# First attention of a two-layer transformer: order of the score and weighting steps on TensorE, and the normalisation on VectorE

## The chip, the cores and the metric

The kernel runs on one core of one Trainium2 chip. The metric is the device time of one execution in microseconds (us).

## The reference, cut to what matters

The whole program is two layers, each an attention and a feed-forward part. The change touches the first attention alone: 16 heads of width 16, two batches of 2048 tokens, causal.

```python
q, k, v = heads(x @ Wq.T), heads(x @ Wk.T), heads(x @ Wv.T)
scores = jnp.einsum('bhqd,bhkd->bhqk', q, k) / sqrt(d_k) + mask
attn = jax.nn.softmax(scores, axis=-1)
out = jnp.einsum('bhqk,bhkd->bhqd', attn, v)
```

## The kernel before, in words

`phase_attention` works through eight units. A unit is four heads of one batch. Inside a unit the 2048 queries are four slices of 512 (q = 0 to 3), and the keys are tiles of 128 (t). By causality slice q needs key tiles 0 to 4q+3, so a unit has 4+8+12+16 = 40 steps (q, t), numbered g = 0 to 39. The last four steps of a slice lie on the diagonal. There the first `off` = 0, 128, 256, 384 columns are masked in full and are left out, so these four steps are 512, 384, 256 and 128 queries wide. All other steps are 512 wide. A slice edge is therefore a passage from the narrowest step to a full one: g3 to g4, g11 to g12, g23 to g24, and g39 to g0 of the next unit.

Each step does this:

- TensorE computes scores in two pairs of heads (p = 0, 1), two matmuls a pair, into one of three `ps_s` buffers (L758). Pair s = 2*step+p may start once the exponential of pair s-3 has released its buffer.
- ScalarE takes the exponential of a pair, 128 x up to 1024 elements, from PSUM into one of four `probs` buffers (L710). A step's first exponential waits for the weighting of the step four back.
- On diagonal steps GpSimd zeroes the triangle of the 128 x 128 block in all four heads (L698).
- TensorE "weighs": it multiplies probs by V with a column of ones, four heads side by side, and accumulates in `ps_o[:, q % 2]` (L775). Row 16 of each head's 32 rows is the sum of the exponentials.

At the end of a slice VectorE copies `ps_o` to `weighted` (L723), splits it into a high and a low part (L725, L727). TensorE spreads the sums over the rows of their head by two matmuls into the same `ps_o` buffer (L788, L789). VectorE takes the reciprocal (L730), multiplies (L732) and splits the result (L736, L738). SyncE writes it out. The first weighting of slice n waits for VectorE's reading of the spread totals of slice n-2, which held the same `ps_o` buffer.

Nothing schedules this: each engine's order is written out in Python. On TensorE the order is set by `LAG = 2`: scores of step `at`, weighting of step `at - 2`, and the spread of a slice that ended at step `at - 4`.

```python
for at in range(len(STEPS) + LAG + 2):
    if at < len(STEPS):
        scores(at)
    if 0 <= at - LAG < len(STEPS):
        weigh(at - LAG)
    if at - LAG - 2 >= 0:
        u, g = STEPS[at - LAG - 2]
        if g in LAST:
            spread_denominators(u, LAST.index(g))
```

Of the kernel before, what the change touches and what calls it, by code (L numbers as in the profile page):

```python
# [15 lines left out]
P = 128  # L16
# [5 lines left out]
BT = TB * P  # L22
# [9 lines left out]
HALF = 64  # L32
STACK_ROWS = 3 * DH
SHIFT_PARTS = 2
USED_ROWS = STACK_ROWS + SHIFT_PARTS
# [25 lines left out]
def sems(k, stem, names):  # L61
    return [sem(k, f"{stem}_{n}") for n in names.split()]
# [547 lines left out]
def phase_attention(k):  # L610
# [6 lines left out]
    TILE_LIST = [(q, t, max(0, (t - TB * q) * P)) for q in range(SLICES) for t in range(TB * (q + 1))]  # L617
    NT = len(TILE_LIST)
    LAST = [max(g for g, (q, _, _) in enumerate(TILE_LIST) if q == s) for s in range(SLICES)]
    DIAG = [g for g, (q, t, _) in enumerate(TILE_LIST) if t >= TB * q]  # L620
    STEPS = [(u, g) for u in range(UNITS) for g in range(NT)]
    SCORE_BUFS, PROB_BUFS = 3, 4
    LAG = 2
    LOADS = STACK_LOADS + 2
    ROWS_OUT = 2 * HG

    with ExitStack() as mem:
        def sb(name, shape, dt):
            return mem.enter_context(nc.sbuf_tensor(name, shape, dt))

        Q, K = ((k["first_stacks"][n], sb(name, [P, 2, SEQ], F32R)) for n, name in enumerate(("Q_odd", "K_odd")))
# [3 lines left out]
        inv = sb("inv_denominator", [P, BT], F32)  # L635
# [4 lines left out]
        ps_s = mem.enter_context(nc.psum_tensor("ps_s", [P, SCORE_BUFS, 2, BT], F32))  # L640
        ps_o = mem.enter_context(nc.psum_tensor("ps_o", [P, 2, BT], F32))
# [3 lines left out]
        ones_in, pick_ok, zero_ok, scores_ok, exp_ok, mask_ok, pv_ok, sums_ok, picked_ok, norm_ok, result_ok = sems(  # L645
            k, "attention", "ones_in pick_ok zero_ok scores_ok exp_ok mask_ok pv_ok sums_ok picked_ok norm_ok result_ok")

        def group_and_batch(u):
            return u % GROUPS, u // GROUPS

        with nc.Block() as block:
# [14 lines left out]
            @block.sync  # L666
            def _(sp):
                load_shifts(sp, 0, 0)
                load_ones(sp, io, K[1], ones_in)
                load(sp, 1, 1)  # L670
                for u in range(UNITS):
                    g, b = group_and_batch(u)
                    for q in range(SLICES):
                        sp.wait_ge(result_ok, SLICES * u + q + 1)
                        for n, out in enumerate((out_hi, out_lo)):
                            for h in range(HG):
                                row = HG * DH * g + DH * h
                                sp.dma_start(io["attended"][n, b, row:row + DH, q * BT:(q + 1) * BT],
                                             out[32 * h:32 * h + DH, q % 2].bitcast(F32)).then_inc(stored[q % 2], 16)
                    if u + 2 < UNITS:  # L680
                        sp.wait_ge(scores_ok, 2 * NT * (u + 1))
                        load(sp, u + 2, u % 2)
                for j in range(2):
                    sp.wait_ge(stored[j], 16 * ROWS_OUT * (SLICES // 2 * UNITS))
# [28 lines left out]
            @block.vector  # L713
            def _(dve):
                dve.memset(ps_o[:, :, :], 0.0).then_inc(zero_ok, 1)
                dve.sem_inc(loaded[0], 16 * STACK_LOADS)
                dve.wait_ge(pick_ok, 2)
                dve.tensor_copy(pick[:, :, :], pick_f32[:, :, :]).then_inc(pick_ok, 1)
                for u in range(UNITS):
                    for q in range(SLICES):  # L720
                        n = SLICES * u + q
                        dve.wait_ge(pv_ok, NT * u + LAST[q] + 1)
                        dve.tensor_copy(sums[:, q % 2], ps_o[:, q % 2]).then_inc(sums_ok, 1)  # L723
                        dve.wait_ge(sums_ok, 3 * n + 1)
                        dve.tensor_copy(sums_hi[:, :], sums[:, q % 2]).then_inc(sums_ok, 1)  # L725
                        dve.wait_ge(sums_ok, 3 * n + 2)
                        dve.tensor_tensor(sums_lo[:, :], sums[:, q % 2], sums_hi[:, :].bitcast(F32), ALU.subtract  # L727
                                          ).then_inc(sums_ok, 1)
                        dve.wait_ge(picked_ok, n + 1)
                        dve.reciprocal(inv[:, :], ps_o[:, q % 2]).then_inc(norm_ok, 1)  # L730
                        dve.wait_ge(norm_ok, 3 * n + 1)
                        dve.tensor_tensor(result[:, :], sums[:, q % 2], inv[:, :], ALU.mult).then_inc(norm_ok, 1)  # L732
                        dve.wait_ge(norm_ok, 3 * n + 2)
                        if n >= 2:
                            dve.wait_ge(stored[q % 2], 16 * ROWS_OUT * (n // 2))
                        dve.tensor_copy(out_hi[:, q % 2], result[:, :]).then_inc(norm_ok, 1)  # L736
                        dve.wait_ge(norm_ok, 3 * n + 3)
                        dve.tensor_tensor(out_lo[:, q % 2], result[:, :], out_hi[:, q % 2].bitcast(F32), ALU.subtract  # L738
                                          ).then_inc(result_ok, 1)

            @block.tensor
            def _(pe):
                pe.wait_ge(zero_ok, 1)

                def scores(at):
                    u, g = STEPS[at]
                    j = u % 2
                    q, t, off = TILE_LIST[g]
                    if g == 0:
                        pe.wait_ge(loaded[j], 16 * LOADS * (u // 2 + 1))  # L750
                        if u == 1:
                            pe.wait_ge(ones_in, 32)
                    for p in range(2):
                        s = 2 * at + p
                        if s >= SCORE_BUFS:
                            pe.wait_ge(exp_ok, s - SCORE_BUFS + 1)
                        for h in range(2):
                            last = pe.matmul(ps_s[:, s % SCORE_BUFS, h, off:BT],  # L758
                                             K[j][HALF * h:HALF * h + USED_ROWS, p, t * P:(t + 1) * P],
                                             Q[j][HALF * h:HALF * h + USED_ROWS, p, q * BT + off:(q + 1) * BT],  # L760
                                             start=True, stop=True)
                        last.then_inc(scores_ok, 1)

                def weigh(at):
                    u, g = STEPS[at]
                    q, t, off = TILE_LIST[g]
                    group, b = group_and_batch(u)
                    n = SLICES * u + q
                    if t == 0 and n >= 2:
                        pe.wait_ge(norm_ok, 3 * (n - 2) + 1)  # L770
                    pe.wait_ge(exp_ok, 2 * at + 2)
                    if g in DIAG:
                        pe.wait_ge(mask_ok, len(DIAG) * u + DIAG.index(g) + 1)
                    for h in range(HG):
                        last = pe.matmul(ps_o[32 * h:32 * h + DH + 1, q % 2, off:BT],  # L775
                                         k["V"][:, group, SEQ_TILES * b + t, h, :],
                                         probs[:, at % PROB_BUFS, h, off:BT],
                                         start=(t == 0), stop=(g == LAST[q]))
                    last.then_inc(pv_ok, 1)

                def spread_denominators(u, q):

                    n = SLICES * u + q
                    if n == 0:
                        pe.wait_ge(pick_ok, 3)
                    pe.wait_ge(sums_ok, 3 * n + 3)
                    rows = pick[:, :, :].rearrange("p h r -> p (h r)")
                    pe.matmul(ps_o[:, q % 2], rows, sums_hi[:, :], start=True, stop=False)  # L788
                    pe.matmul(ps_o[:, q % 2], rows, sums_lo[:, :], start=False, stop=True).then_inc(picked_ok, 1)  # L789

                for at in range(len(STEPS) + LAG + 2):
                    if at < len(STEPS):
                        scores(at)
                    if 0 <= at - LAG < len(STEPS):
                        weigh(at - LAG)
                    if at - LAG - 2 >= 0:
                        u, g = STEPS[at - LAG - 2]
                        if g in LAST:
                            spread_denominators(u, LAST.index(g))

# [1333 lines left out]
```

## Time and profile before

| quantity | value |
|---|---|
| median of 3 runs | 1855.95 us (1855.9 to 1857.81) |
| the profiled execution | 1856.14 us |
| its span, first to last instruction | 1854.3 us |
| mean granted TensorE clock, of full speed | 0.943 |
| first attention: first and last exponential | 124.3 us and 672.3 us of the span |
| busy in the whole span: TensorE, ScalarE, VectorE, GpSimd | 88%, 52%, 50%, 25% |

The span is read from the first to the last instruction; the profiled execution took 1.8 us more. The first attention is 548 us of it. Times in the rows further down count from the start of the span.

### The profile page before, as it was taken

What the parts mean: (1) busy time and instruction counts of PE and PEld (TensorE: products, weight loads), DVE (VectorE), ACT (ScalarE), POOL (GpSimd) and SP (SyncE); (2) the same over time, 40 slices, a digit from 0 to 9 for tenths busy, and PEclk for the clock granted to TensorE, in tenths of its full rate; (3) what the DMA queues carried; (4) which work ended last, traced back from release to release, by engine and by line L of the source; (5) the groups of instructions that cost most, each with busy time, mean ns of one, the idle gap of its engine ahead of it and who ended that gap; (6) DMA issues with size and microseconds to landing.
All of it is one profiled execution on the core that took longest, in us unless ns stands there. A gap on an engine that the chain in (4) does not pass through costs nothing. (4 is left out here: it accounts for less than half of the span.)

```text
span 1854.3 us, 30959 instructions
## 1 busy us (share of the span) xinstructions
PE 1626.1 (88%) x10275; PEld 1110.3 (60%) x10276; DVE 922.7 (50%) x1795; ACT 962.0 (52%) x1531; POOL 457.7 (25%) x500
## 2 busy tenths in 40 slices
PE   7769999999999957999559999999668987997998
PEld 5632322322322316888548888888567976896887
DVE  6524433443443436777553333333375554755785
ACT  5459999999999944443332222222133334333332
POOL 0001111210210201555542222222153003001674
PEclk9979999999999987999879999999878997998999
DMA  8991405514514029221231111111212010000001
GB/s 274 268 254 28 86 14 88 87 24 77 87 30 70 18 62 308 79 80 46 76 107 50 50 50 51 51 51 51 88 46 91 1 57 1 1 1 4 24 23 46
DMA packets 79647, 134.44 MB, mean 73 GB/s; under 512 B 11632, under 2 KB 46064, under 8 KB 76400
## 3 DMA queue, kind: packets, MB, share of 16 engines
q1 hardware_dynamic: 72504, 112.00, 23.4%
q0 software_dynamic: 7040, 21.08, 3.6%
q8 instruction: 64, 1.05, 0.2%
q14 instruction: 39, 0.32, 0.1%
HBM read 74.76 MB, written 58.27 MB: 72 GB/s over the span
## 5 line engine op out<-in xcount | busy, mean ns | idle before, releaser
L710 ACT ACTIVATE probs<-ps_s 128x1024 f32<-128x1024 f32 (+3 forms) x640 | 513.8, 954 | 37.2 <-PE ps_s L758 34.2
L775 PE MATMUL ps_o<-probs,V 128*17 128x512 f32 (+3 forms) x2560 | 297.4, 536 | 0.3
L698 POOL TENSOR_SCALAR_AFFINE_SELECT probs<-probs 128x512 f32<-128x512 f32 x128 | 86.8, 680 | 465.5 <-ACT probs L710 461.9
L723 DVE COPY weighted<-ps_o 128x512 f32<-128x512 f32 x32 | 22.1, 690 | 254.7 <-PE ps_o L775 254.7
L1389 DVE COPY slot_hT<-ps_hT 128x512 f32<-128x512 f32 x72 | 49.8, 691 | 196.7 <-PE ps_hT L1432 196.7
L758 PEld LDWEIGHTS ps_s<-Q_even,K_even 50*128 50x128 f32 x640 | 56.1, 186 | 152.1 <-ACT probs L710 130.0
L730 DVE RECIPROCAL inv_denominator<-ps_o 128x512 f32<-128x512 f32 x32 | 107.4, 3358 | 73.8 <-PE ps_o L789 73.8
L758 PE MATMUL ps_s<-Q_even,K_even 50*128 50x512 f32 (+3 forms) x640 | 127.6, 446 | 18.8 <-DMA Q_even<-shift_parts 10.5
L758 PEld LDWEIGHTS ps_s<-Q_odd,K_odd 50*128 50x128 f32 x640 | 55.2, 183 | 140.0 <-ACT probs L710 125.8
L1442 PE MATMUL ps_slot_y<-we_out,slot_hT 128*128 x576 | 136.5, 380 | 1.4 <-DVE slot_hT L1389 0.9
L1922 POOL TENSOR_TENSOR h_lo<-h,h_hi 128x512 fp32r<-128x512 f32 x64 | 89.4, 1413 | 183.8 <-DVE h L1968 183.8
L758 PE MATMUL ps_s<-Q_odd,K_odd 50*128 50x512 f32 (+3 forms) x640 | 126.6, 442 | 7.8 <-ACT probs L710 6.3
L1347 POOL DMA_INDIRECT routed_rows<-slot_y,home_row x72 | 70.3, 977 | 181.5 <-ACT slot_y L1366 176.9
L1808 ACT ACTIVATE probs<-ps_s,neg_row_max 128x512 f32<-128x512 f32 (+2 forms) x80 | 49.3, 623 | 121.2 <-DVE neg_row_max L1770 121.2
L1442 PEld LDWEIGHTS ps_slot_y<-we_out,slot_hT 128*128 128x128 f32 x576 | 103.9, 190 | 13.3 <-issue 2.0
L117 PE MATMUL ps_slot_mid<-we_in_hi,slot_xT_hi 128*128 x144 | 69.6, 483 | 22.8 <-DVE slot_xT_lo L1393 22.8
L775 PEld LDWEIGHTS ps_o<-probs,V 128*17 128x17 f32 x2560 | 42.7, 95 | 77.0 <-issue 63.5
L1371 ACT ACTIVATE slot_silu<-ps_slot_mid 128x512 f32<-128x512 f32 x72 | 43.1, 598 | 80.0 <-PE ps_slot_mid L119 80.0
L1366 ACT ACTIVATE slot_y<-ps_slot_y 128x256 f32<-128x256 f32 x72 | 27.6, 384 | 106.6 <-PE ps_slot_y L1442 106.6
L117 PE MATMUL ps_o<-v_hi,pT_hi 128*128 128x256 f32 x272 | 80.9, 297 | 2.2 <-DVE pT_lo L1775 2.0
L1361 ACT ACTIVATE slot_xT_hi<-ps_xT 128x256 fp32r<-128x256 f32 x72 | 27.6, 384 | 105.1 <-PE ps_xT L1419 105.1
L974 POOL DMA_INDIRECT slots_in<-scaled_rows,slot x64 | 66.3, 1036 | 57.4 <-DVE scaled_rows L1105 42.3
(279 smaller groups left out, 3950.2 us busy)
## 6 DMA issues: line engine op xcount, KB each, us to landing
qk_stacks<-qk_hi SPq DMA_DIRECT2D x64, 256.0 KB, 3.9
slot_rows<-slots_in SPq DMA_DIRECT2D x72, 128.5 KB
qk_stacks<-qk_lo SPq DMA_DIRECT2D x32, 256.0 KB, 3.9
Q_odd<-qk_stacks SPq DMA_DIRECT2D x8, 768.0 KB
K_odd<-qk_stacks SPq DMA_DIRECT2D x8, 768.0 KB
Q_even<-qk_stacks SPq DMA_DIRECT2D x6, 768.0 KB
K_even<-qk_stacks SPq DMA_DIRECT2D x6, 768.0 KB
X<-x SPq DMA_DIRECT2D x8, 512.0 KB, 4.4
```

The source lines that it names most:

```text
L117: pe.matmul(out, lh, rh, start=start, stop=False)
L698: pool.affine_select(out=block_of, in_=block_of, compare_op=ALU.is_ge, fill=0.0, base=0, pattern=[[0, HG], [1, P]], channel_multiplier=-1) ...
L710: act.activation(probs[:, at % PROB_BUFS, 2 * p:2 * p + 2, off:BT], ps_s[:, s % SCORE_BUFS, :, off:BT], ACT.Exp).then_inc(exp_ok, 1)
L730: dve.reciprocal(inv[:, :], ps_o[:, q % 2]).then_inc(norm_ok, 1)
L758: last = pe.matmul(ps_s[:, s % SCORE_BUFS, h, off:BT], K[j][HALF * h:HALF * h + USED_ROWS, p, t * P:(t + 1) * P], Q[j][HALF * h:HALF * h + ...
L775: last = pe.matmul(ps_o[32 * h:32 * h + DH + 1, q % 2, off:BT], k["V"][:, group, SEQ_TILES * b + t, h, :], probs[:, at % PROB_BUFS, h, off ...
L974: pool.indirect_dma_start(out=io["slots_in"], out_offset=bass.IndirectOffsetOnAxis(ap=k["slot"][:, r, TB * b + t:TB * b + t + 1], axis=0), ...
L1347: pool.indirect_dma_start(out=io["routed"], out_offset=bass.IndirectOffsetOnAxis(ap=home[:, j], axis=0), in_=y[:, j, :], in_offset=None).t ...
L1389: dve.tensor_copy(hT[:, :, :], ps_h[:, :, :]).then_inc(hT_ok, 1)
L1442: last = pe.matmul(ps_y[:, :], hT[:, f], wo[:, bass.ds(e, 1), f, :], start=(f == 0), stop=(f == FC - 1))
L1808: act.activation(probs[:, q % 2, g * P:(g + m) * P], ps_s[:, g * P:(g + m) * P], ACT.Exp, bias=neg_top[:, q:q + 1], accum_out=chunk_total[ ...
L1922: pool.tensor_tensor(h_lo[:, j, f], h[:, f % 2], h_hi[:, j, f].bitcast(F32), ALU.subtract).then_inc(lo_ok, 1)
```

## The change

It does two things. On TensorE, `LAG` is replaced by a table: before the weighting of step `at`, scores are issued up to pair 2*at+1 plus 4 where the step is 512 or 128 wide, and plus 6 where it is 384 or 256 wide. The spread of a slice stays two weightings behind its last one. On VectorE, the spread totals are first copied from PSUM to SBUF (`inv_denominator`), and the reciprocal is taken in place from the copy; the semaphore that releases the `ps_o` buffer is raised by the copy.

```diff
-    LAG = 2
+    LEAD = {0: 4, P: 6, 2 * P: 6, 3 * P: 4}
+    SPREAD_AFTER = 2
...
-                        dve.reciprocal(inv[:, :], ps_o[:, q % 2]).then_inc(norm_ok, 1)
-                        dve.wait_ge(norm_ok, 3 * n + 1)
+                        dve.tensor_copy(inv[:, :], ps_o[:, q % 2]).then_inc(norm_ok, 1)
+                        dve.wait_ge(norm_ok, 4 * n + 1)
+                        dve.reciprocal(inv[:, :], inv[:, :]).then_inc(norm_ok, 1)
+                        dve.wait_ge(norm_ok, 4 * n + 2)
...
-                        pe.wait_ge(norm_ok, 3 * (n - 2) + 1)
+                        pe.wait_ge(norm_ok, 4 * (n - 2) + 1)
...
-                for at in range(len(STEPS) + LAG + 2):
+                scored = 0
+                for at in range(len(STEPS) + SPREAD_AFTER):
                     if at < len(STEPS):
-                        scores(at)
-                    if 0 <= at - LAG < len(STEPS):
-                        weigh(at - LAG)
-                    if at - LAG - 2 >= 0:
-                        u, g = STEPS[at - LAG - 2]
+                        for s in range(scored, min(2 * at + 2 + LEAD[TILE_LIST[STEPS[at][1]][2]], 2 * len(STEPS))):
+                            scores(s)
+                            scored = s + 1
+                        weigh(at)
+                    if at >= SPREAD_AFTER:
+                        u, g = STEPS[at - SPREAD_AFTER]
```

TensorE's order before, at the start of a unit, from the scores of g2 (256 wide) to those of g6. `ps_s` rows are scores, `ps_o` rows with `probs` are weightings, L788 and L789 the spread of the last slice of the unit before.

```order
L758 MATMUL ps_s<-Q_odd,K_odd 128x256 x4
L775 MATMUL ps_o<-probs,V 17x512 x4
L758 MATMUL ps_s<-Q_odd,K_odd 128x128 x4
L775 MATMUL ps_o<-probs,V 17x384 x4
L788 MATMUL ps_o<-weighted_hi,denominator_pick 128x512
L789 MATMUL ps_o<-weighted_lo,denominator_pick 128x512
L758 MATMUL ps_s<-Q_odd,K_odd 128x512 x4
L775 MATMUL ps_o<-probs,V 17x256 x4
L758 MATMUL ps_s<-Q_odd,K_odd 128x512 x4
L775 MATMUL ps_o<-probs,V 17x128 x4
L758 MATMUL ps_s<-Q_odd,K_odd 128x512 x4
```

The same place in the changed kernel, where the same lines are L760, L777, L790 and L791:

```order
L760 MATMUL ps_s<-Q_odd,K_odd 128x256 x4
L777 MATMUL ps_o<-probs,V 17x512 x4
L760 MATMUL ps_s<-Q_odd,K_odd 128x128 x4
L760 MATMUL ps_s<-Q_odd,K_odd 128x512 x4
L777 MATMUL ps_o<-probs,V 17x384 x4
L790 MATMUL ps_o<-weighted_hi,denominator_pick 128x512
L791 MATMUL ps_o<-weighted_lo,denominator_pick 128x512
L760 MATMUL ps_s<-Q_odd,K_odd 128x512 x4
L777 MATMUL ps_o<-probs,V 17x256 x4
L777 MATMUL ps_o<-probs,V 17x128 x4
L760 MATMUL ps_s<-Q_odd,K_odd 128x512 x4
```

The scores of g4, the first full step of the next slice, have moved ahead of the weighting of g1 and of the spread; those of g5 ahead of the weighting of g2; and the weightings of g2 and g3 now follow each other. The same happens at the other three slice edges, where no spread stands in between. Away from the edges the order is the old one.

VectorE's order for one slice, in the changed kernel:

```order
L724 COPY weighted<-ps_o 128x512 [waits attention_pv_ok]
L726 CAST weighted_hi<-weighted 128x512 [waits attention_sums_ok]
L728 TENSOR_TENSOR weighted_lo<-weighted,weighted_hi 128x512 [waits attention_sums_ok]
L731 COPY inv_denominator<-ps_o 128x512 [waits attention_picked_ok]
L733 RECIPROCAL inv_denominator<-inv_denominator 128x512 [waits attention_norm_ok]
L735 TENSOR_TENSOR attention_result<-weighted,inv_denominator 128x512 [waits attention_norm_ok]
L739 CAST attention_hi<-attention_result 128x512 [waits attention_norm_ok]
```

Before, one RECIPROCAL from `ps_o` (L730) stood where the COPY and the RECIPROCAL now are; the rest is as it was.

## Rows read from the trace of the kernel before

**Rows 1.** Busy time by stretch: window, PE, PEld, DVE, ACT, POOL, clock, DMA share, GB/s.
```profile
124.30:193.50 69.20, 67.01 (x472) 20.22 (x470) 21.25 (x21) 64.22 (x81) 10.64 (x16) 0.95 0.31 53
330.60:399.00 68.40, 66.04 (x490) 20.30 (x488) 28.14 (x28) 64.22 (x80) 10.93 (x17) 1.00 0.38 63
```
**Rows 2.** The page's groups: line, operation, count | busy, mean ns | idle before, releaser.
```profile
L710 ACT ACTIVATE probs<-ps_s 128x1024 f32<-128x1024 f32 (+3 forms) x640 | 513.8, 954 | 37.2 <-PE ps_s L758 34.2
...
L723 DVE COPY weighted<-ps_o 128x512 f32<-128x512 f32 x32 | 22.1, 690 | 254.7 <-PE ps_o L775 254.7
...
L730 DVE RECIPROCAL inv_denominator<-ps_o 128x512 f32<-128x512 f32 x32 | 107.4, 3358 | 73.8 <-PE ps_o L789 73.8
```
**Rows 3.** ScalarE's waits, 330.6 to 399: total us, times, longest.
```profile
ACT probs L710 <- PE ps_s L758: 3.8, 5, 1.4
```
**Rows 4.** Timeline of ScalarE around 349 us: start us, us, line, operation, count, idle before.
```profile
347.48 1.81 ACT L710 ACTIVATE probs<-ps_s 128x768 f32<-128x768 f32 x3
349.39 0.66 ACT L710 ACTIVATE probs<-ps_s 128x256 f32<-128x256 f32 x2
350.70 1.02 ACT L710 ACTIVATE probs<-ps_s 128x1024 f32<-128x1024 f32 x1 [0.65 <-PE ps_s L758]
```
**Rows 5.** Timeline of TensorE around 349 us.
```profile
349.33 0.84 PE L775 MATMUL ps_o<-probs,V 128*17 128x384 f32 x8
```
**Rows 6.** Timeline of TensorE in the unit's first 14 us.
```profile
334.58 0.44 PE L758 MATMUL ps_s<-Q_odd,K_odd 50*128 50x128 f32 x4
335.04 0.84 PE L775 MATMUL ps_o<-probs,V 128*17 128x384 f32 x8
335.81 0.50 PE L788 MATMUL ps_o<-weighted_hi,denominator_pick 128*128 128x512 f32 x1
336.47 0.73 PE L758 MATMUL ps_s<-Q_odd,K_odd 50*128 50x512 f32 x4
...
343.69 0.50 PE L788 MATMUL ps_o<-weighted_hi,denominator_pick 128*128 128x512 f32 x1 [0.40 <-DVE weighted_lo L727]
```
**Rows 7.** Timeline of ScalarE around 335 us.
```profile
333.80 1.12 ACT L710 ACTIVATE probs<-ps_s 128x512 f32<-128x512 f32 x2
335.01 0.38 ACT L710 ACTIVATE probs<-ps_s 128x256 f32<-128x256 f32 x1
337.07 1.02 ACT L710 ACTIVATE probs<-ps_s 128x1024 f32<-128x1024 f32 x1 [1.41 <-PE ps_s L758]
```
**Rows 8.** Timeline of VectorE from the reciprocal of the unit before.
```profile
336.58 3.36 DVE L730 RECIPROCAL inv_denominator<-ps_o 128x512 f32<-128x512 f32 x1 [2.18 <-PE ps_o L789]
...
341.77 0.68 DVE L723 COPY weighted<-ps_o 128x512 f32<-128x512 f32 x1
```
**Rows 9.** Single lines of VectorE: duration ns min/median/max, first and last start.
```profile
L1793 DVE RECIPROCAL inv_row_sum<-row_sum x32: 163/164/166, 1395.9 to 1695.3; 128x1 f32<-128x1 f32 x32
...
L215 DVE RECIPROCAL ln_rstd<-ln_std x32: 166/170/180, 9.9 to 1815.6; 128x4 f32<-128x4 f32 x32
...
L725 DVE CAST weighted_hi<-weighted x32: 426/426/428, 134.7 to 674.3; 128x512 fp32r<-128x512 f32 x32
...
L736 DVE CAST attention_hi<-attention_result x32: 426/428/740, 143.1 to 680.4; 128x512 fp32r<-128x512 f32 x32
```
**Rows 10.** Timeline of TensorE in unit 0.
```profile
129.38 0.69 PE L758 MATMUL ps_s<-Q_even,K_even 50*128 50x128 f32 x4
130.00 1.48 PE L775 MATMUL ps_o<-probs,V 128*17 128x384 f32 x8
```
**Rows 11.** Timeline of ScalarE in unit 0, after the same scores.
```profile
132.03 3.77 ACT L710 ACTIVATE probs<-ps_s 128x1024 f32<-128x1024 f32 x4 [1.47 <-PE ps_s L758]
```
**Rows 12.** Timeline of VectorE at the end of the attention.
```profile
676.29 3.36 DVE L730 RECIPROCAL inv_denominator<-ps_o 128x512 f32<-128x512 f32 x1 [0.82 <-PE ps_o L789]
...
693.52 0.43 DVE L152 CAST wo_hi<-silu 128x512 fp32r<-128x512 f32 x1 [11.96 <-DMA router_raw<-router]
```
**Rows 13.** Timeline of GpSimd at the next diagonal.
```profile
346.97 0.63 POOL L698 TENSOR_SCALAR_AFFINE_SELECT probs<-probs 128x512 f32<-128x512 f32 x1 [10.60 <-ACT probs L710]
```

More of the change, by code:

```diff
@@ L729, in _ @@
                         dve.wait_ge(picked_ok, n + 1)
-                        dve.reciprocal(inv[:, :], ps_o[:, q % 2]).then_inc(norm_ok, 1)
-                        dve.wait_ge(norm_ok, 3 * n + 1)
+                        dve.tensor_copy(inv[:, :], ps_o[:, q % 2]).then_inc(norm_ok, 1)
+                        dve.wait_ge(norm_ok, 4 * n + 1)
+                        dve.reciprocal(inv[:, :], inv[:, :]).then_inc(norm_ok, 1)
+                        dve.wait_ge(norm_ok, 4 * n + 2)
                         dve.tensor_tensor(result[:, :], sums[:, q % 2], inv[:, :], ALU.mult).then_inc(norm_ok, 1)
-                        dve.wait_ge(norm_ok, 3 * n + 2)
+                        dve.wait_ge(norm_ok, 4 * n + 3)
                         if n >= 2:
@@ L736, in _ @@
                         dve.tensor_copy(out_hi[:, q % 2], result[:, :]).then_inc(norm_ok, 1)
-                        dve.wait_ge(norm_ok, 3 * n + 3)
+                        dve.wait_ge(norm_ok, 4 * n + 4)
                         dve.tensor_tensor(out_lo[:, q % 2], result[:, :], out_hi[:, q % 2].bitcast(F32), ALU.subtract
@@ L743, in _, with scores @@
                 pe.wait_ge(zero_ok, 1)
-                def scores(at):
+                def scores(s):
+                    at, p = s // 2, s % 2
                     u, g = STEPS[at]
@@ L748, in scores @@
                     q, t, off = TILE_LIST[g]
-                    if g == 0:
+                    if g == 0 and p == 0:
                         pe.wait_ge(loaded[j], 16 * LOADS * (u // 2 + 1))
@@ L752, in scores @@
                             pe.wait_ge(ones_in, 32)
[L753 to L762, printed above, removed]
+                    if s >= SCORE_BUFS:
+                        pe.wait_ge(exp_ok, s - SCORE_BUFS + 1)
+                    for h in range(2):
+                        last = pe.matmul(ps_s[:, s % SCORE_BUFS, h, off:BT],
+                                         K[j][HALF * h:HALF * h + USED_ROWS, p, t * P:(t + 1) * P],
+                                         Q[j][HALF * h:HALF * h + USED_ROWS, p, q * BT + off:(q + 1) * BT],
+                                         start=True, stop=True)
+                    last.then_inc(scores_ok, 1)
                 def weigh(at):
```

## The prediction

> **What bounds the kernel now.** The change touches one stage, so I first read the busy times by stretch [rows 1]. The second row is one unit of the first attention: in 68.40 us ScalarE is busy 64.22 and TensorE 66.04. TensorE's figure overstates it, because overlapping matmuls are counted from start to modelled end. Its clock is at 1.00, the 2.4 GHz level, in that unit and at 0.95 in unit 0. Next the page's groups [rows 2]: the exponentials at L710 stand for 513.8 us, and ScalarE idles 37.2 us before them, nearly all for scores at L758. That makes ScalarE the bound, with its stalls as the prize. ScalarE's waits show how few they are: 5 in one unit, 3.8 us together, the longest 1.4 [rows 3]. Four stand where a slice's narrow steps end, and the fifth at the second slice's last full step. All work between them runs at ScalarE's own pace, and the change does not alter it.
>
> **Part 1, scores earlier at a slice edge.** I take the edge from g11 to g12. The last narrow exponential starts at 349.39+0.66-0.38 = 349.67, with 0.38 for one of them [rows 7]; the two start 0.66-0.38 = 0.28 apart. The next, g12's first, starts only at 350.70 [rows 4]. Its own buffer had been released when g10's second exponential ended, at 347.48+1.81 = 349.29. Between the two stands the weighting of g9, which TensorE started at 349.33 for 0.84 us [rows 5]. Now the scores go first. One pair takes 0.50, as a spread matmul of the same 512 columns does, and ScalarE follows 0.10 later: g4's scores start at 336.47, and 336.47+0.50 = 336.97 stands against its exponential at 337.07 [rows 6, 7]. From a release to the start of what waits for it I allow 0.05 (my estimate; VectorE's reciprocal follows the spread by 0.04). So 349.29+0.65 = 349.94. ScalarE itself could start 0.28 after 349.67, at 349.95. So g12 starts at 349.95 instead of 350.70, which is 0.75 us less. The edges into g24 and into g0 of the next unit show the same wait of 0.65. Over 8 units that is 8 + 8 + 7 = 23 edges: 23 x 0.75 = **-17.3 us**.
>
> Does the wait come back one step later? g13's first exponential needs a free `probs` buffer, that is the weighting of g9, which now stands behind g12's scores. It ended at 350.17 [rows 5], and even 1 us later it ends before 351.8, when g13's exponential is due (349.95 + 2 x 0.92; four full ones take 3.77 with 1.02 for one, so they follow each other every 0.92 [rows 4, 11]). I count nothing for it.
>
> **Part 2, the edge from g3 to g4.** Here the spread of the unit before stands in the queue too, and ScalarE waits longest, 1.41 us [rows 7]. Now g4's scores need only the release by g2's second exponential at 333.80+1.12 = 334.92, so its first exponential starts at about 335.57 instead of 337.07. This gain does not last: g8, the last full step of this slice, is held from the other side. Its scores stand behind the spread of slice 0, and that spread waits 0.40 us for VectorE [rows 6]. VectorE is late because it still works on the slice before: the reciprocal starts at 336.58, and only when three more operations are done does it copy slice 0, at 341.77 [rows 8]. What decides g8 is thus how VectorE's chain moves, by two terms.
>
> First, the chain starts later. The spread moves behind g4's scores. These end at about 335.95 (the release by g3's first exponential at 335.01+0.38, plus 0.05, plus 0.50). The weighting of g1 then takes 0.84 and the spread 0.73, with each start 0.07 ahead of the end before it, as 335.81 is of 335.04+0.84 = 335.88; so the spread ended at 336.47+0.07 = 336.54, 0.73 after its start [rows 6]. Now: 335.95-0.07+0.84-0.07+0.73 = 337.38, against 336.54. That is +0.84 us.
>
> Second, the chain changes length. A copy from PSUM costs 0.69 [rows 2] and the wait between the two some 0.035 (an estimate, after the 0.04 from 336.54 to the reciprocal's start at 336.58 [rows 8]). The reciprocal from PSUM took 3.36. **The price of a reciprocal from SBUF at this width is not in the trace**, and it decides the case. The upper end is that it costs the same, 3.36. The lower end comes from the small ones: 164 ns for one element, 170 for four [rows 9], so 2 ns for each further element where the PSUM form needs (3358-164)/511 = 6.25; 164+511 x 2 = 1.19 us. At 6.25 ns per element the four-element form would take 183 ns, and none of its 32 runs took over 180. A middle value comes from copies: from PSUM 690 ns [rows 2], as a cast between SBUF tensors 426 [rows 9], so about half per element once a fixed part of some 160 is taken off. Half of the reciprocal's element time gives 164+3194/2 = 1761 ns. I take 1.76: it lies nearer to the small rows than the upper end does. The Trainium skill agrees with the halving: "VectorE: DVE Perf Modes", section "Why PSUM operands drop a tier", says that the doubled two-port mode needs both SBUF read ports and PSUM has one. It names no reciprocal, so it does not settle whether this operation has such a mode; if none, the sum is that of the second rival.
>
> With 1.76 the chain is 0.69+0.035+1.76-3.36 = -0.87, and -0.87+0.84 = -0.03: g8 starts where it did. In units 1 to 7: 7 x -0.03 = **-0.2 us**.
>
> **Unit 0** has no chain before it and a low clock at its start. The scores of g3 end at 130.07, and those of g4 stand behind a weighting of 1.48 [rows 10]; g4's exponential starts at 132.03 [rows 11]. Without that weighting in front, its scores take some 0.7 from 130.0: 130.85. That is **-1.2 us**, and nothing at g8 takes it back.
>
> **The tail.** After the last exponential comes one more chain, and everything after it waits: VectorE next works after 11.96 us, on a load of the following stage [rows 12]. The shorter chain counts once: **-0.9 us**.
>
> The release of `ps_o` by the copy instead of the reciprocal I cost at nothing: no row shows TensorE waiting for L730. It matters in the new order only as protection. SyncE's loads for a later unit wait for scores that now come a little earlier, and have a unit's time. GpSimd's order is unchanged.
>
> Sum: -17.3 -0.2 -1.2 -0.9 = -19.6, on the profiled 1856.14, which is 0.2 above the median 1855.95. By the edges' start-gaps alone (0.65 instead of 0.75) it would be -17.3, and I lean a little that way: **1837.0 us**, 1.0% faster.
>
> **Rivals.**
>
> 1. *The reciprocal from SBUF costs the same, 3.36.* For: its arithmetic is the same, and the small rows are mostly fixed cost. Against: the four-element row. Then each of 7 chains and the tail is 1.6 longer: 8 x 1.6 = 12.8. The q1 slice loses 1.57 us where the other three edges gain 2.25. 1837.0+12.8 = 1849.8.
> 2. *GpSimd is held up.* The select of g8 starts at 346.97 [rows 13], and the new reciprocal of slice 0 runs from about 345.2 (343.69+0.73 for the spread, 0.04, 0.69 and 0.035) to 346.9, so they could meet. L736, a cast between SBUF tensors, once took 740 ns instead of 428 [rows 9]; something can hold such operations. If the select waits half of a reciprocal, 0.9, and its weighting has 0.2 to spare, 7 units lose 0.7: 1842. The Trainium skill's "SBUF — State Buffer", section "SBUF: two separate sides", gives the rule: a VectorE operation in a two-port mode and a GpSimd one exclude each other for a whole instruction.
> 3. *Slower: the stalls at the edges stay, while the chain grows.* Place: g13, g25, g5 and g1, where the exponential waits for the `probs` buffer of a weighting that has moved behind a pair of score steps. If these waits take the place of the 0.75, and the reciprocal costs 3.36, each of units 1 to 7 loses 0.84+0.73 = 1.57 at g8 and the tail 0.7: 1856+11.7 = 1867.7. It decides from the point where the edges together give less than 1.6 per unit. Against it: the 1 us to spare, worked out above.
> 4. *The edges give nothing and the reciprocal costs 1.76*: only unit 0 and the tail remain, 1854.
>
> **How the numbers follow.** A measurement of this kernel can tell about 0.2%, 3.7 us, from no change. Chances: forecast 0.64, rival 1 0.20, rival 2 0.06, rival 3 0.05, rival 4 0.05. The forecast's own range is 1832.5 (reciprocal at 1.19: 8 x 0.57 = 4.6 less) to 1841. To leave out no more than 2 in 10 the range goes over rivals 1 and 2: 1832.5 to 1850.5. Faster: the forecast, rivals 2 and nearly all of 1 = 0.88; same: rival 4 and a rest of 1 = 0.07; slower: rival 3 = 0.05.
>
> **What would show it.** The reciprocal's row reads 1.2 to 1.8 us (right) or 3.36 (rival 1). The exponentials at g12, g24 and g0 have no idle before them; ScalarE's waits in a unit fall from 5 to about 1 or 2, with one left at g8 and one at g5, where g5's scores stand behind the spread. The unit's period falls from 68.4 to about 66.2 us. The prediction is wrong if an idle shows at g13 or g25, if selects of 1.2 us and more appear at L698 in every unit, or if the period stays above 68.

## The result, and the profile after

| | before | changed |
|---|---|---|
| median of 12 runs each | 1856.66 us (1852.46 to 1860.52) | 1865.17 us (1860.98 to 1870.33) |
| span of the profiled execution | 1854.3 us | 1863.6 us |
| end of the first attention's last exponential | 672.3 us | 679.8 us |

The ratio is 1.0049, with a 95% interval of 1.0037 to 1.0061. The change made the kernel slower by 0.5%. The forecast was 1837.0 us, with a range of 1832.5 to 1850.5.

The page's groups of the changed kernel, against [rows 2]:

```profile
L711 ACT ACTIVATE probs<-ps_s 128x1024 f32<-128x1024 f32 (+3 forms) x640 | 513.7, 953 | 45.1 <-PE ps_s L760 42.6
...
L733 DVE RECIPROCAL inv_denominator<-inv_denominator 128x512 f32<-128x512 f32 x32 | 107.3, 3353 | 1.1
```

ScalarE's work is the same, but its idle time before it has grown from 37.2 to 45.1 us, and the part of it that is for scores from 34.2 to 42.6. The reciprocal takes 3353 ns from SBUF where it took 3358 from PSUM. It is not cheaper.

ScalarE's waits in unit 3 (330.8 to 400.1), against [rows 3]:

```profile
ACT probs L711 <- PE ps_s L760: 4.8, 4, 3.6
```

Before, five waits of at most 1.4 us made up 3.8 us. Now one wait of 3.6 us outweighs the ones that have gone. Its place is g8, as ScalarE's timeline shows (start us, us, line, operation, count, idle before):

```profile
347.27 1.94 ACT L711 ACTIVATE probs<-ps_s 128x1024 f32<-128x1024 f32 x2 [3.63 <-PE ps_s L760]
349.75 2.56 ACT L711 ACTIVATE probs<-ps_s 128x768 f32<-128x768 f32 x4 [0.53 <-PE ps_s L760]
```

Behind it stand further waits at g9 and g11, which the kernel before did not have, and ahead of it one of 0.40 us at g5. At the edges into g12, g24 and g0 nothing is left, and none at g4 either. Each of these rows begins in the narrow steps and runs on into the full ones (into g0, g12 and g24) with no idle time between, where [rows 4] had 0.65:

```profile
330.07 4.48 ACT L711 ACTIVATE probs<-ps_s 128x256 f32<-128x256 f32 x7
...
352.86 8.71 ACT L711 ACTIVATE probs<-ps_s 128x256 f32<-128x256 f32 x10
...
372.59 4.05 ACT L711 ACTIVATE probs<-ps_s 128x256 f32<-128x256 f32 x5
```

VectorE's timeline at that place, against [rows 8]:

```profile
337.54 0.69 DVE L731 COPY inv_denominator<-ps_o 128x512 f32<-128x512 f32 x1 [2.19 <-PE ps_o L791]
338.27 3.35 DVE L733 RECIPROCAL inv_denominator<-inv_denominator 128x512 f32<-128x512 f32 x1
...
343.45 0.68 DVE L724 COPY weighted<-ps_o 128x512 f32<-128x512 f32 x1
344.17 0.43 DVE L726 CAST weighted_hi<-weighted 128x512 fp32r<-128x512 f32 x1
344.63 0.69 DVE L728 TENSOR_TENSOR weighted_lo<-weighted,weighted_hi 128x512 fp32r<-128x512 f32 x1
```

TensorE's timeline next to it, against [rows 6]:

```profile
341.38 1.05 PE L777 MATMUL ps_o<-probs,V 128*17 128x512 f32 x8
345.37 0.64 PE L790 MATMUL ps_o<-weighted_hi,denominator_pick 128*128 128x512 f32 x1 [2.94 <-DVE weighted_lo L728]
345.82 0.63 PE L791 MATMUL ps_o<-weighted_lo,denominator_pick 128*128 128x512 f32 x1
346.38 1.22 PE L760 MATMUL ps_s<-Q_odd,K_odd 50*128 50x512 f32 x4
347.52 1.75 PE L777 MATMUL ps_o<-probs,V 128*17 128x512 f32 x8
```

TensorE idles 2.94 us before the spread of slice 0, where it idled 0.40. And then its work is slower than it was: 0.64 and 0.63 for the two matmuls of the spread instead of 0.50 and 0.40, 1.22 for two score pairs instead of 0.73, 1.75 for a weighting instead of 1.05. The busy times by stretch say why (columns as in [rows 1], the clock third from the end). The first three rows are unit 3, the last three the same place in unit 4:

```profile
342.40:345.40 3.00, 0.06 (x5) 0.03 (x1) 2.82 (x5) 1.24 (x2) 0.00 (x0) 1.00 0.12 27
345.40:349.20 3.80, 3.80 (x14) 0.97 (x14) 2.68 (x2) 1.93 (x2) 0.00 (x0) 0.55 0.41 97
349.20:353.00 3.80, 3.67 (x34) 1.27 (x30) 3.48 (x4) 2.99 (x7) 2.17 (x3) 1.00 1.03 177
...
413.80:414.70 0.90, 0.02 (x1) 0.02 (x1) 0.79 (x2) 0.00 (x0) 0.00 (x0) 0.52 0.30 71
414.70:418.50 3.80, 3.80 (x14) 1.13 (x14) 2.52 (x2) 1.77 (x2) 0.00 (x0) 0.50 0.45 104
418.50:422.30 3.80, 3.80 (x28) 1.09 (x24) 3.70 (x4) 2.33 (x5) 1.27 (x2) 0.72 1.02 153
```

In the 3 us of the wait TensorE did nothing. In unit 3 the granted clock still read 1.00 there; in the 3.8 us after it, when the work came, it read 0.55, close to the lower level of 1.2 GHz, and then 1.00 again. Units 1, 5 and 7 look the same. In units 2, 4 and 6 the low reading began while TensorE was still waiting (0.52 in the last 0.9 us of the wait in unit 4) and reached into the second 3.8 us after it (0.72). The Trainium skill's "Advanced Engine Details and Errata", section "Clock Domains", says that the array's clock is gated to 1.2 GHz when idle. The rows agree on the level and on what came before it; they also show the full clock for most of the idle time and the low one mostly for the work behind it.

The time from the first exponential of a unit to that of the next was 68.40 us in the mean of units 1 to 7 and is 69.84, between 69.29 and 70.73 (for the last unit, to its last exponential). The longer ones are units 2, 4 and 6. 7 x 1.44 is 10.1 us. Unit 0, which has no chain before it, fell from 69.15 to 66.68. What follows the last exponential is 1.7 us longer, 0.7 of it the added copy. 10.1-2.5+1.7 = 9.3, the difference of the spans. The 1.7 cannot be put down to the change as a whole: in the profiled executions of the kernels below, which do not differ behind the attention, that part took between 1177.1 and 1184.3 us.

### The profile page after: what moved, and what is told of

Read it like the earlier page. It is cut to its first block and busy times, and to the rows that moved or that the text cites. A ratio compares the mean times of both kernels' runs of the same rounds, so it can differ in the third digit from the quotient of the medians.

```text
span 1863.6 us, 30991 instructions
## 1 busy us (share of the span) xinstructions
PE 1632.2 (88%) x10275; PEld 1116.9 (60%) x10276; DVE 947.7 (51%) x1827; ACT 961.8 (52%) x1531; POOL 454.7 (24%) x500
## 3 DMA queue, kind: packets, MB, share of 16 engines
q8 instruction: 64, 1.05, 0.2%
## 5 line engine op out<-in xcount | busy, mean ns | idle before, releaser
L711 ACT ACTIVATE probs<-ps_s 128x1024 f32<-128x1024 f32 (+3 forms) x640 | 513.7, 953 | 45.1 <-PE ps_s L760 42.6
L777 PE MATMUL ps_o<-probs,V 128*17 128x512 f32 (+3 forms) x2560 | 297.9, 547 | 0.1
L760 PEld LDWEIGHTS ps_s<-Q_even,K_even 50*128 50x128 f32 x640 | 57.4, 193 | 141.5 <-ACT probs L711 119.1
L760 PE MATMUL ps_s<-Q_even,K_even 50*128 50x512 f32 (+3 forms) x640 | 127.8, 457 | 12.3 <-DMA Q_even<-shift_parts 10.9
L760 PEld LDWEIGHTS ps_s<-Q_odd,K_odd 50*128 50x128 f32 x640 | 55.8, 187 | 127.9 <-ACT probs L711 114.6
L760 PE MATMUL ps_s<-Q_odd,K_odd 50*128 50x512 f32 (+3 forms) x640 | 125.2, 447 | 0.7
L733 DVE RECIPROCAL inv_denominator<-inv_denominator 128x512 f32<-128x512 f32 x32 | 107.3, 3353 | 1.1
L777 PEld LDWEIGHTS ps_o<-probs,V 128*17 128x17 f32 x2560 | 45.9, 96 | 83.8 <-issue 59.2
L978 POOL DMA_INDIRECT slots_in<-scaled_rows,slot x64 | 66.0, 1031 | 57.7 <-DVE scaled_rows L1109 42.6
```

The lines of the kernel that those rows point to most:

```text
L711: act.activation(probs[:, at % PROB_BUFS, 2 * p:2 * p + 2, off:BT], ps_s[:, s % SCORE_BUFS, :, off:BT], ACT.Exp).then_inc(exp_ok, 1)
L733: dve.reciprocal(inv[:, :], inv[:, :]).then_inc(norm_ok, 1)
L760: last = pe.matmul(ps_s[:, s % SCORE_BUFS, h, off:BT], K[j][HALF * h:HALF * h + USED_ROWS, p, t * P:(t + 1) * P], Q[j][HALF * h:HALF * h + ...
L978: pool.indirect_dma_start(out=io["slots_in"], out_offset=bass.IndirectOffsetOnAxis(ap=k["slot"][:, r, TB * b + t:TB * b + t + 1], axis=0), ...
```

## The experiments

Theory A, formed from these rows: the new order does what was forecast at the edges, but VectorE's chain of copy and reciprocal makes TensorE wait at the spread of slice 0, and behind this wait the clock falls. Its rival B: the new order by itself delays g8, and the copy is a bystander.

Periods are means over units 1 to 7, read like those above. Each median was taken on the same chip as runs of the kernel before, and is to be read by its ratio to them. The kernel before took 1855.4 us beside the order alone, the copy alone, the half reciprocal and the ten widths; 1854.0 beside the first busy attempt, the two kernels with five weightings and the kernel before with the later spread; 1852.75 beside the three quarters, the second busy attempt, the four weightings and the three from PSUM.

**The order alone.** The changed kernel with the old reciprocal.

```diff
-dve.tensor_copy(inv[:, :], ps_o[:, q % 2]).then_inc(norm_ok, 1)
-dve.wait_ge(norm_ok, 4 * n + 1)
-dve.reciprocal(inv[:, :], inv[:, :]).then_inc(norm_ok, 1)
-dve.wait_ge(norm_ok, 4 * n + 2)
+dve.reciprocal(inv[:, :], ps_o[:, q % 2]).then_inc(norm_ok, 1)
+dve.wait_ge(norm_ok, 3 * n + 1)
```

> The new TensorE order with the old reciprocal straight from PSUM. Theory A (VectorE's chain holds the spread of slice 0, and TensorE's long wait there drops its clock): the chain starts 0.84 us later but is not longer, so the unit's period is 68.4-2.25+0.84 = 67.0 us, TensorE waits under 1 us before that spread because the weighting of g4 now waits for the reciprocal, the clock stays at 1.00 in the units, and the whole takes about 1844 us. Theory B (the new order by itself delays g8, the copy is a bystander): as the changed kernel, 1862 us or more.

Measured: 1844.5 us, ratio 0.9939 (0.9919 to 0.9959), period 67.17. TensorE's timeline, and the stretch of unit 3:

```profile
337.58 1.05 PE L775 MATMUL ps_o<-probs,V 128*17 128x512 f32 x8 [1.35 <-DVE inv_denominator L731]
...
341.29 0.50 PE L788 MATMUL ps_o<-weighted_hi,denominator_pick 128*128 128x512 f32 x1 [1.01 <-DVE weighted_lo L728]
```

```profile
327.30:394.40 67.10, 64.71 (x490) 20.64 (x490) 28.94 (x28) 64.14 (x81) 10.67 (x17) 1.00 0.40 65
```

The first weighting of slice 1 does wait for the whole reciprocal, 1.35 us. The early release by the copy takes that wait away. But two short waits, 1.35 and 1.01 us, stand here in the place of one long one, g8 comes earlier, and the clock stays at 1.00. ScalarE idles 0.73 us at g7 behind the first of them and 1.45 at g8. That the first costs nothing here, because g8 would only wait the longer for the spread, is argued and not shown. B falls.

**The copy alone.** The old order with the copy and the SBUF reciprocal, the first half of the diff.

> The old TensorE order with the copy and the reciprocal from SBUF. Theory A: the chain is 0.72 us longer in 7 units and at the tail, 8 x 0.72 = 5.8 us: about 1862 us if the clock stays at 1.00, more if the wait before the spread (0.40+0.72 = 1.1 us) is enough to drop it. Theory B: nothing but the tail, 1857 us.

Measured: 1861.8 us, ratio 1.0030 (1.0017 to 1.0044), period 69.12, which is 0.72 above 68.40. The spread's row:

```profile
344.72 0.50 PE L790 MATMUL ps_o<-weighted_hi,denominator_pick 128*128 128x512 f32 x1 [1.11 <-DVE weighted_lo L727]
```

The wait grew from 0.40 to 1.11 us and the matmul behind it still takes 0.50. The 0.7 us of the copy pass straight through to the end of each unit. B had expected no more than the tail's share, 1857.

**The price that the prediction had taken.** The changed kernel with a reciprocal of half the columns; the other half is multiplied by the totals themselves.

```diff
-dve.reciprocal(inv[:, :], inv[:, :]).then_inc(norm_ok, 1)
+dve.reciprocal(inv[:, :BT // 2], inv[:, :BT // 2]).then_inc(norm_ok, 1)
```

> The changed kernel with the reciprocal over the first 256 of 512 columns only; the other columns are multiplied by the totals themselves. The reciprocal should take about 1.76 us, the price that the prediction had taken. Theory A: the spread of slice 0 is then on time, the clock stays, and the sum of the prediction comes true: period about 66.1 to 66.4 us, 1837 to 1840 us in all. Theory B (the order delays g8): 1855 us or more.

Measured: 1838.4 us, ratio 0.9903 (0.9880 to 0.9926), period 66.51. The reciprocal's row (ns min/median/max) and unit 3:

```profile
L733 DVE RECIPROCAL inv_denominator<-inv_denominator x32: 1753/1753/1755, 138.6 to 660.9; 128x256 f32<-128x256 f32 x32
```

```profile
323.10:389.30 66.20, 64.81 (x490) 20.71 (x488) 25.29 (x32) 64.00 (x81) 10.54 (x17) 1.00 0.40 65
```

With the price taken for the reciprocal, the prediction's sum comes out: it had 1837.0, a ratio of 0.990. The mean period is 66.51, and 66.30 without the last of the seven units, which took 67.7. Its spread, with times as long as in the changed kernel:

```profile
601.17 0.66 PE L790 MATMUL ps_o<-weighted_hi,denominator_pick 128*128 128x512 f32 x1 [1.35 <-DVE weighted_lo L728]
601.63 0.63 PE L791 MATMUL ps_o<-weighted_lo,denominator_pick 128*128 128x512 f32 x1
```

The granted clock read 0.55 over the 3.8 us from this row's start. So a wait of 1.35 us was enough there, while the six units before had waits as long (7 waits, 9.5 us in all) and kept the clock.

**Is any width cheaper?** The SBUF reciprocal in ten pieces.

```diff
-dve.reciprocal(inv[:, :], inv[:, :]).then_inc(norm_ok, 1)
+at = 0
+for width in (256, 128, 64, 32, 16, 8, 4, 2, 1, 1):
+    last = dve.reciprocal(inv[:, at:at + width], inv[:, at:at + width])
+    at += width
+last.then_inc(norm_ok, 1)
```

> The changed kernel with its SBUF reciprocal in ten pieces of 256, 128, 64, 32, 16, 8, 4, 2, 1 and 1 columns. If an element costs 6.25 ns at every width: 1757, 957, 557, 357, 257, 207, 182, 170 and 164 ns. If short ones are cheaper, as the row of four elements (170 ns) suggested: clearly less below 16 columns. The time of the whole is not the question; it should be a few us above the changed kernel's.

The groups by form (busy us, mean ns of one):

```profile
L735 DVE RECIPROCAL inv_denominator<-inv_denominator 128x256 f32<-128x256 f32 x32 | 56.1, 1753 | 1.1
L735 DVE RECIPROCAL inv_denominator<-inv_denominator 128x128 f32<-128x128 f32 x32 | 28.6, 895 | 0.0
...
L735 DVE RECIPROCAL inv_denominator<-inv_denominator 128x1 f32<-128x1 f32 x64 | 6.5, 143 | 0.0
L735 DVE RECIPROCAL inv_denominator<-inv_denominator 128x16 f32<-128x16 f32 x32 | 6.2, 195 | 0.0
L735 DVE RECIPROCAL inv_denominator<-inv_denominator 128x8 f32<-128x8 f32 x32 | 4.6, 145 | 0.0
L735 DVE RECIPROCAL inv_denominator<-inv_denominator 128x2 f32<-128x2 f32 x32 | 4.3, 134 | 0.0
L735 DVE RECIPROCAL inv_denominator<-inv_denominator 128x4 f32<-128x4 f32 x32 | 3.8, 120 | 0.0
```

From 4 to 8 columns 25 ns, from 8 to 16 columns 50, from 16 to 128 columns 700: 6.25 ns for each element from 4 columns up, the PSUM form's figure. What differs is the fixed part: 95 ns behind another reciprocal with no wait between, about 150 for the first piece, which waits. The expectation had one fixed part for all; from 128 down to 4 columns its figures are too high by some 60. Below 4 columns the rule does not hold: pieces of 2 and of 1 took 134 and 143 ns, more than the piece of 4, and no run says why. At 6.25 ns per element the 170 ns for four elements and the 164 for one [rows 9] leave fixed parts of 145 and 158, so their difference says nothing of the element's cost.

The whole took 1859.9 us in its one run, 4.5 above the kernel before, where a few us above the changed kernel had been expected; a single run does not tell these apart. Its waits before the spread were 3.16 us, and the clock fell behind all seven.

**Three quarters.** As the half, but over 384 columns, to see whether the cost grows in step with the chain.

> The changed kernel with the reciprocal over 384 of 512 columns (2.55 us), the other columns multiplied by the totals themselves; TensorE's wait before the spread is then about 2.1 us instead of 2.9. If the cost is the chain alone, the period is 66.2+0.8 = 67.0 us and the whole 1844 to 1846 us. If the wait of 2.1 us is enough to make the clock fall, the period is 68 us and more and the whole over 1850 us.

Measured: 1855.4 us, ratio 1.0010 (0.9996 to 1.0024), period 68.78. TensorE:

```profile
344.47 0.58 PE L790 MATMUL ps_o<-weighted_hi,denominator_pick 128*128 128x512 f32 x1 [2.15 <-DVE weighted_lo L728]
344.85 0.63 PE L791 MATMUL ps_o<-weighted_lo,denominator_pick 128*128 128x512 f32 x1
```

The reciprocal took 2.55 us, 0.8 more than the half, yet the period rose by 2.3. The cost is not in step with the chain: behind a wait of 2.15 us the matmuls were slow, in all seven units.

**Busy in the wait, first attempt.** Ten small matmuls of constants before each spread, once VectorE has copied out the buffer that the spread overwrites.

```diff
+pe.wait_ge(sums_ok, 3 * n + 1)
 rows = pick[:, :, :].rearrange("p h r -> p (h r)")
+for _ in range(10):
+    pe.matmul(ps_o[:, q % 2, 0:P], rows, rows, start=True, stop=True)
 pe.wait_ge(sums_ok, 3 * n + 3)
```

> The changed kernel; before each spread TensorE runs ten small matmuls of constants into the buffer that the spread will overwrite, as soon as VectorE has copied it out, so that its idle time before the spread of slice 0 falls from 2.9 us to under 2. Theory A (the fall of the clock behind the long wait costs what arithmetic at full speed does not explain): the clock stays at 1.00, the spread takes 0.73 us again, the period is 68.4-2.25+1.57 = 67.7 us and the whole about 1849 us. Theory C (the extra time has another cause): about 1865 us as before.

Measured: 1893.5 us, ratio 1.0208 (1.0181 to 1.0236), far above both expectations.

```profile
356.14 1.92 PE L791 MATMUL ps_o<-denominator_pick 128*128 128x128 f32 x10 [1.76 <-DVE weighted L724]
357.86 0.73 PE L793 MATMUL ps_o<-weighted_hi,denominator_pick 128*128 128x512 f32 x1
```

The extra matmuls stand before all four spreads of a unit. Before the spread of the last slice they start VectorE's chain about 1.1 us later, and before the others they hold the scores behind them. Before the spread of slice 0 they could begin only after 1.76 us of idling, and the spread behind them was slow all the same. It does not decide between the theories, since an idle time was left; it adds 1.76 us to the idle times behind which the clock fell, in all seven units.

**Busy in the wait, second attempt.** Only before the spread of slice 0 in units 1 to 7, and with work that waits for nothing else by then: g8's first score pair, eleven times over, into its own buffer, which is free.

```diff
+if q == 0 and u > 0:
+    s = 2 * (NT * u + LAST[q] + 5)
+    pe.wait_ge(exp_ok, s - SCORE_BUFS + 1)
+    for _ in range(11):
+        for h in range(2):
+            pe.matmul(ps_s[:, s % SCORE_BUFS, h, 0:BT],
+                      K[u % 2][HALF * h:HALF * h + USED_ROWS, 0, 4 * P:5 * P],
+                      Q[u % 2][HALF * h:HALF * h + USED_ROWS, 0, BT:2 * BT],
+                      start=True, stop=True)
 pe.wait_ge(sums_ok, 3 * n + 3)
```

> The changed kernel; in units 1 to 7, between the weighting of g5 and the spread of slice 0, TensorE computes the first score pair of g8 eleven times over into the buffer it will use anyway (about 2.7 us of matmuls), so that it waits as long but is not idle. Theory A (the clock falls behind the idle wait): clock 1.00 in the units, the spread takes 0.73 us again, period 67.7 to 67.9 us, about 1850 us in all. Theory C (the time beyond the chain's 1.57 us has another cause): 1865 us.

Measured: 1847.8 us, ratio 0.9973 (0.9961 to 0.9986), period 67.89.

```profile
340.29 2.79 PE L793 MATMUL ps_s<-Q_odd,K_odd 50*128 50x512 f32 x22
343.31 0.50 PE L799 MATMUL ps_o<-weighted_hi,denominator_pick 128*128 128x512 f32 x1 [0.24 <-DVE weighted_lo L728]
343.64 0.40 PE L800 MATMUL ps_o<-weighted_lo,denominator_pick 128*128 128x512 f32 x1
343.97 0.73 PE L760 MATMUL ps_s<-Q_odd,K_odd 50*128 50x512 f32 x4
344.63 1.05 PE L777 MATMUL ps_o<-probs,V 128*17 128x512 f32 x8
```

```profile
328.60:396.40 67.80, 67.52 (x512) 22.70 (x512) 31.80 (x32) 64.02 (x81) 10.48 (x17) 1.00 0.38 64
```

This is the changed kernel plus 2.79 us of useless matmuls a unit, and it is faster than both kernels. The spread waits for VectorE as long as before; all durations behind it are the full-speed ones. Against the changed kernel the period falls from 69.84 to 67.89: the low clock costs 1.95 us a unit, 13.7 in seven. Unit by unit it is 1.5 us in units 1, 3, 5 and 7 and 2.4 to 2.7 in units 2, 4 and 6, where the low reading lasted longer.

**The spread of slice 0 later.** If no scores stand behind the wait, neither cost should arise. Five weightings after its slice instead of two:

```diff
-    SPREAD_AFTER = 2
+    SPREAD_AFTER = (5, 2, 2, 2)
...
-                    if at >= SPREAD_AFTER:
-                        u, g = STEPS[at - SPREAD_AFTER]
-                        if g in LAST:
-                            spread_denominators(u, LAST.index(g))
+                    for q, after in enumerate(SPREAD_AFTER):
+                        if 0 <= at - after < len(STEPS) and STEPS[at - after][1] == LAST[q]:
+                            spread_denominators(STEPS[at - after][0], q)
```

> The changed kernel with the spread of slice 0 issued five weightings after its slice instead of two, so that no scores stand behind TensorE's wait for VectorE. Theory A: the stall at g8 is gone, the clock stays; what is left is 0.2 us at each last diagonal step, some 0.5 at g5 and 0.1 at g16 and g28: period about 64.6 us, in all 1826 to 1830 us. Rival: VectorE's chain is a bound of its own and the stall only moves to a later step, 1850 us or more.

Measured: 1839.1 us, ratio 0.9908 (0.9881 to 0.9935), period 66.25. The stall at g8 went and the clock stayed, but 1.6 us a unit more were left than expected. The rival was partly right. ScalarE idles 0.76 us at g11, the narrowest step, which stands behind the spread in its new place. And VectorE's chain for slice 0 now runs into the end of slice 1, whose copy starts late, at 347.00, and the wait is at the next spread, which costs ScalarE 0.79 us at g16:

```profile
348.93 0.50 PE L790 MATMUL ps_o<-weighted_hi,denominator_pick 128*128 128x512 f32 x1 [0.74 <-DVE weighted_lo L728]
```

**The same with the reciprocal from PSUM.**

> As the late spread, with the old reciprocal from PSUM: the first weighting of slice 1 now waits for the whole reciprocal. If the early release by the copy is worth something, this is 0.5 to 0.9 us a unit slower than the late spread with the copy, less 0.7 at the tail: 1830 to 1834 us. If it is worth nothing, the shorter chain makes it equal or 0.7 us faster.

Measured: 1835.5 us, ratio 0.9900 (0.9876 to 0.9923), period 66.35, 0.1 more than with the copy; the intervals of the two ratios overlap. The stall of 0.79 us at g16 is gone, and ScalarE idles instead at g7, behind the weighting that waits for the reciprocal:

```profile
337.11 6.16 ACT L711 ACTIVATE probs<-ps_s 128x1024 f32<-128x1024 f32 x8 [0.72 <-PE ps_s L758]
```

So at this place the copy's early release and its length cancel.

**The kernel before with the later spread.** Its spread of slice 0 three weightings later, order and reciprocal as they were.

> The kernel before, with the spread of slice 0 three weightings later and nothing else. Theory A: only the 0.45 us idle at g8 goes, 0.55 us a unit in 7 units: 1851 to 1853 us. Rival: the spread in its new place disturbs the narrow steps and gives it back, no change.

Measured: 1854.0 us, ratio 1.0000 (0.9984 to 1.0016), period 68.51. The rival was right: the idle at g8 went, and a new one of 0.76 us came at the narrowest step, g11, behind the spread:

```profile
353.12 0.66 ACT L710 ACTIVATE probs<-ps_s 128x256 f32<-128x256 f32 x2 [0.76 <-PE ps_s L758]
```

**Four weightings, with the copy,** `SPREAD_AFTER = (4, 2, 2, 2)`:

> The changed kernel with the spread of slice 0 four weightings after its slice. The sums are then ready when TensorE comes to it, and VectorE is free again before slice 1 ends: g8 is not held, g16 not either, the narrow steps lose some 0.4 us at g10. Period about 65.2 us, 1830 to 1833 us. If the stall at g16 that five weightings brought (0.8 us) stays, 66 us and 1838.

Measured: 1834.55 us, ratio 0.9897 (0.9880 to 0.9914), period 65.30, as expected. ScalarE's waits in unit 3:

```profile
ACT probs L711 <- PE ps_s L760: 0.9, 3, 0.4
```

The total is 1.6 us over the expectation's upper end. In the profiled execution unit 0 took 68.85 us against 66.68 in the changed kernel, and its low clock at the start lasted longer. Unit 0 varies: in the kernels with the new order and the spread in its first place it took 65.7 to 67.9 us, the first busy attempt aside. So it is a likely source of the excess and not a shown one.

**Three weightings, from PSUM,** `SPREAD_AFTER = (3, 2, 2, 2)`:

> The reciprocal from PSUM, the new order, and the spread of slice 0 three weightings after its slice. The sums are ready at that point; left are the stalls at g5 (0.5) and g7 (0.8, the weighting of g4 waits for the reciprocal): period about 66.2 us, 1833 to 1837 us, no slower than five weightings with the same reciprocal (1835.5 us).

Measured: 1834.8 us, ratio 0.9907 (0.9887 to 0.9927), period 66.10. The wait of the first weighting for the reciprocal, 1.3 us, is still there. The ratios of the last two kernels and of the two with five weightings, 0.9897 to 0.9908, cannot be told apart; each is about 1% faster than the kernel before. The period can: 65.30 with the copy and four weightings, 66.10 to 66.35 for the three others.

## Why the prediction was wrong, point by point

- **What bounds the kernel**: right. ScalarE's busy time did not change; its stalls moved and grew.
- **Part 1, 0.75 us at an edge**: right in place and size. In the changed kernel slices 2 and 3 of unit 3 take 19.73 and 27.06 us where they took 20.48 and 27.83, and slice 0 takes 5.07 instead of 5.72 (to the end of the last exponential each). No wait came back at g13 or g25, so the returning stalls of rival 3 did not occur, though the kernel is slower as rival 3 had it. Its other part, a chain that starts 0.84 us later and is longer by the copy, did occur.
- **Part 2, the first term**, the chain's later start of 0.84 us: right. VectorE's reading of the spread totals starts 6.83 us into unit 3 where it started at 5.99. With the order alone the period is 67.17, and 68.40-2.25+0.84 = 66.99.
- **Part 2, the second term, is the first step that failed**: "Half of the reciprocal's element time gives 164+3194/2 = 1761 ns. I take 1.76". It takes 3353 ns. With the copy in front the chain is 0.72 us longer and not 0.87 shorter, so g8 could not start where it did: its first exponential comes 16.56 us into unit 3 instead of 14.37. The step inferred an element's cost from two short instructions whose fixed parts differ, and from a copy's behaviour. The Trainium skill's rule on PSUM operands ("VectorE: DVE Perf Modes", section "Why PSUM operands drop a tier") fits the copy from PSUM at 690 ns beside the cast between SBUF tensors at 426, which are two different operations. The reciprocal gains nothing in SBUF, 3353 against 3358 ns; the section names no reciprocal, and the runs decide.
- **Rival 1 priced the second failure wrongly**: with 3.36 it gave 1849.8 us, still faster than before. What it left out is the low clock. The wait behind which the clock falls was in reach: the prediction knew of a wait of 0.40 us at the spread, and with rival 1's chain that wait had to grow by about 2.5 us, since TensorE also reached it earlier. It never asked how fast TensorE works after an idle time that long. Rival 1 with the clock kept is the second busy attempt, ratio 0.9973; 1849.8 against 1856.1 is 0.9966.
- **Unit 0 and the tail**: -2.5 measured, where -1.2 and two edges of 0.75 gave -2.7. With unit 0 varying by some 2 us between kernels that differ little there, so close a match is partly luck. The tail lost 0.7 by the copy instead of gaining 0.9.
- **Rival 2, GpSimd held up**: not seen. With the reciprocal in SBUF its select still takes 634 ns in the median.

So of the prediction's three mechanisms, two stood as worked out: the edges and the chain's later start. The reciprocal's price turned the forecast of -19 us into about -6, and the low clock added 13.7. That gives about +7.5, where the medians differ by 8.5.

Periods of 69.3 to 69.6 and of 70.2 to 70.7 alternate, and the longer ones are those in which the low reading lasted longer. What decides how long it lasts stays open. That the fall as such follows from idling is shown by the second busy attempt; which idle lengths are safe is not. The fall was seen behind the waits of 3.16, 2.94, 2.15 and 1.76 us in all seven units; behind waits of about 1.35 us in one unit of the half reciprocal, and in none of the order alone or of the two later spreads with the reciprocal from PSUM; behind those of 1.11 in none.

## What to carry to other kernels

A change that lets TensorE run ahead also lets it reach its next wait sooner. Work out how long it will stand idle there, and price the low clock behind the wait as well as the wait. Place an instruction that depends on another engine's chain where that chain has ended, but not so late that the next chain starts late: here two weightings gave 1.0049 of the time before, and four and five gave 0.9897 and 0.9908, with periods of 65.30 and 66.25 us. And take an element's cost only from two widths of the same instruction in the same position.

## What the runs showed of the hardware

- VectorE's reciprocal costs 6.25 ns per element of a partition in SBUF from 4 columns up, and takes as long from PSUM as from SBUF, 3358 and 3353 ns for 512. Pieces of 4 to 128 columns that follow each other without a wait have a fixed part of about 95 ns; the first piece, which waits, has about 150.
- Behind an idle wait of 2.94 us the granted clock reads 0.55 or 0.50 over 3.8 us of work, and a full weighting takes 1.75 instead of 1.05 us. During the idle time itself it still reads 1.00 in unit 3; in units 2, 4 and 6 the low reading began within the last 0.9 to 1.2 us of it.
- Filling such a wait with 2.79 us of repeated matmuls kept the clock at 1.00, and took the changed kernel from 1.0049 to 0.9973 of the time before.
